# Paged attention with a low-rank layer behind it: value products one pair later, reordered transfers, and 14 of 16 pages on the sync queue

## The chip, the cores and the metric

One NeuronCore of one Trainium2 chip. The time is device microseconds of one execution; less is better. The host only lays arrays out.

## The reference, cut to what matters

```python
# x (32, 32, 512); block table (32, 16) of pages 0..63; cached lengths 207..1644; language ids
B, S, HID = 32, 32, 512;  D, HQ, HK = 128, 32, 8;  PAGES, PSIZE, NPP = 64, 32, 16
q = rope(rmsnorm(x @ Wq.T, q_norm_w), pos);  k = rope(rmsnorm(x @ Wk.T, k_norm_w), pos);  v = x @ Wv.T
kc = k_cache[block_table].reshape(B, 512, HK, D);  vc = v_cache[block_table].reshape(B, 512, HK, D)
k_all, v_all = concat([kc, k], 1), concat([vc, v], 1)          # 544 keys; each KV head serves 4 query heads
scores = einsum('bqhd,bkhd->bhqk', q, k_all) / sqrt(D), cached keys past the length masked
x = x + (softmax(scores) @ v_all).reshape(B, S, HQ * D) @ Wo.T
# second layer: x + x @ W.T + 2 * sum over the top 2 of 8 experts of gate * (x @ A_e.T) @ B_e.T
```

## The kernel before

The 1024 rows of x are cut into 8 tiles of 128 rows (4 batch rows of 32 tokens each), the 8 KV heads into 4 groups of 2. `walk` (L59) runs the same body for each group g and tile t: tiles 0, 6 and 7 are written out, tiles 1 to 5 are a loop, and groups 0 to 2 are a loop around these. So there are 32 bodies, i = 8g + t. In a body there are 8 pairs p (a batch row b = p // 2 and a KV head h = p % 2), each with 4 query heads x 32 tokens = 128 query rows.

Products that need float32 accuracy are made of three passes over operands split into a high and a low part (`three_pass`, L187, whose products all have L193): ACT writes the rounded high part and DVE the rest.

What each engine does in a body:

- PE, for p = 0 to 6: `turn_probs(i, p)` (transposes of the probabilities into PT, L537 and L538), `score(i, p + 2)` into SX, a piece of the projections of the next tile (`fill`: K and V's block 0, query blocks 1 and 2), in some steps a transpose of cached keys (`turn_unit`), of the new queries (`turn_q`) or keys (`turn_k`), then `weigh(i, p)`: eight products of cached values (L550) and two of the tile's own values (L554), which use only the 32 partitions of row b, into O. Then come pair 7 and the output projection `project_out` in two halves, with score 0 and 1 of the next tile between them.
- ACT copies the turned probabilities to SBUF (`take_pT`, L772, one buffer pT), takes exponents (L776), evacuates projections, squares for the norm, and rounds weights (`round_weights`, at the steps of `HI_AT`). It issues 4 of every row's 16 page fetches (L267).
- DVE masks and takes the minimum (L992), normalises (L999), makes the rope products (L975, L979), the low parts of weights at the steps of `LO_AT`, splits O, and adds y (`add_y`, L1027).
- POOL makes the norm factor and finishes the rope (L1258 to L1278), keeps the tile's own values (`keep_v`, L1286), and issues the value gathers, 16 indirect DMAs a tile (L1225).
- SP issues every other transfer, in the written order of its body (L384 to L465): y of the tile (L402), register loads of page addresses (`read_pages`, L319), 12 of every row's 16 key pages for the next tile (`load_pages`, L323 to L326; `fetch_page`, L264), x, masks, halves of weights (`next_half`, L304), cached keys in (`load_kn`) and turned keys out (`store_unit`) for the next group, and last the store of y, for which it waits for `y_added` (L462 to L464).

The cached keys of a group are turned and split once, in 8 units of 8 pages, one unit per tile, and stored to `kT_pages` in DRAM; pages are fetched from there, 64 KB each, by an address in a register. Addresses for all tiles sit in `pages` on one partition, and DVE adds one group's bytes once a group. Row b of the next tile may be fetched once this tile's scores of the row are done (`s_done`). Halves of weights go through two staging buffers.

The order of the work is thus written out by hand: which step each job sits in on each engine, and the order of SP's transfers. All cross-engine order is by semaphores that count up; a queue blocks at the first one that isn't reached.

## Time and profile before

| | us |
|---|---|
| runs shown, median (lowest, highest) | 1611.72 (1608.89, 1619.95) |
| the profiled execution | 1600.16 |
| its span on the engines | 1598.3 |
| PE, POOL, DVE, ACT busy | 1379.9, 948.5, 823.5, 662.0 |
| mean granted TensorE clock | 0.923 of full speed |

The span is from the first to the last instruction of the profiled execution; 1.9 us of its time lie outside. Engine names: PE is TensorE (matmuls), PEld its weight loads, DVE VectorE, ACT ScalarE, POOL GpSimd, SP SyncE; SPq and ACTq are their sequencers, which issue DMAs. "L267" is a line of the kernel above. "xN" is a count, "idle before" the engine's idle time just before an instruction and what ended it. The clock column (PEclk) is a mean of stretches at either 1.0 (2.4 GHz) or 0.5 (1.2 GHz). Waits are put down to what came last.

### The profile page before, as it was taken

Reading aid. Unit: us, or ns where it says so; the run is one execution under the profiler, and the core shown is the slowest. Engines: PE = TensorE matmul, PEld = TensorE weight load, DVE = VectorE, ACT = ScalarE, POOL = GpSimd, SP = SyncE. Lnnn points to the kernel's source line nnn. Section 1 sums busy time; section 2 is a strip of 40 time slices with the busy share of each in tenths; the row PEclk is TensorE's granted clock in tenths of the full one; section 3 lists DMA queues with packets and bytes.
Section 4 is the critical chain, followed back from the end, with each engine's and each line's share of the span. In section 5 each row is a group of like instructions: output and inputs, shape, how many; then the busy total and the mean of one; then the engine's idle time right before and its main releaser. Section 6 shows DMA issues by size and latency. Waiting matters only on the chain.

```text
span 1598.3 us, 33745 instructions
## 1 busy us (share of the span) xinstructions
PE 1379.9 (86%) x8000; PEld 1171.2 (73%) x8000; DVE 823.5 (52%) x2193; ACT 662.0 (41%) x1742; POOL 948.5 (59%) x1270
## 2 busy tenths in 40 slices
PE   4369999998788999999887999999878989888899
PEld 3258787777676777778676787877767877777777
DVE  5445455455455445555545555545545454545544
ACT  3243444444343344444344444444434344434431
POOL 4446666665565667666555666666655666666500
PEclk9588999898999899999898999999879899989999
DMA  8675766678656676677667666667666565656721
GB/s 293 194 211 156 202 193 199 187 202 246 181 177 182 174 201 190 189 200 212 195 178 212 191 199 197 187 191 222 203 197 183 149 182 165 176 168 174 211 77 53
DMA packets 393726, 299.69 MB, mean 187 GB/s; under 512 B 45905, under 2 KB 349297, under 8 KB 393458
## 3 DMA queue, kind: packets, MB, share of 16 engines
q1 hardware_dynamic: 292386, 193.37, 41.3%
q0 software_dynamic: 24576, 67.14, 14.5%
q10 hardware_dynamic: 76656, 37.98, 8.3%
q8 instruction: 38, 0.62, 0.2%
q14 instruction: 70, 0.57, 0.1%
HBM read 271.27 MB, written 29.13 MB: 188 GB/s over the span
## 4 chain that ended last, share of the span: by engine, by line
PE 42%; issue 16%; SPq 15%; DVE 9%; ACT 4%; DMA 4%; another core or an unknown queue 4%; ACTq 3%; POOL 1%; DVEq 0%; POOLq 0%
PE MISC L193 11%; PE O L550 8%; SPq L267 8%; PE SX L193 6%; PE PROJ L193 5%; PE O L554 4%; PE PT L537 4%; DVE soft L992 2%; ACTq L267 2%; ACT pT L772 2%; DMA stage<-in_wqkv 2%; SPq L319 2%; DVE rope_v L979 2%; SPq L266 1%
## 5 line engine op out<-in xcount | busy, mean ns | idle before, releaser
L1225 POOL DMA_INDIRECT v_rows<-in_kv,step_idx x512 | 506.6, 990 | 195.6 <-issue 132.8
L550 PE MATMUL O<-pT,v_rows 128*128 128x128 f32 x2048 | 304.3, 295 | 132.1 <-ACT pT L772 124.6
L776 ACT ACTIVATE soft<-soft,min_all 128x544 f32<-128x544 f32 x256 | 191.7, 749 | 524.0 <-DVE min_all L992 373.3
L550 PEld LDWEIGHTS O<-pT,v_rows 128*128 128x128 f32 x2048 | 276.2, 205 | 173.8 <-ACT pT L772 154.6
L1008 DVE CAST oT_hi<-O 128x128 fp32r<-128x128 f32 x256 | 73.8, 288 | 409.1 <-PE O L554 303.8
L772 ACT ACTIVATE pT<-PT 128x640 f32<-128x640 f32 x256 | 179.7, 702 | 177.6 <-PE PT L538 103.8
L193 PE MATMUL SX<-kT,qT_hi 128*128 128x288 f32 (+1 forms) x1024 | 242.5, 327 | 8.0 <-DVE qT_lo L1021 3.9
L992 DVE CUSTOM_DVE_ANT_0 soft<-SX,mask 128x544 f32<-128x544 f32 x256 | 184.4, 720 | 52.2 <-PE SX L193 23.8
L193 PEld LDWEIGHTS SX<-kT,qT_hi 128*128 128x128 f32 x1024 | 170.7, 202 | 17.8 <-issue 6.7
L537 PE MATMUL PT<-ident,soft 128*128 128x128 f32 x1024 | 180.7, 303 | 2.1 <-issue 2.1
L999 DVE TENSOR_SCALAR soft<-soft,rden 128x544 f32<-128x544 f32 x256 | 157.4, 615 | 9.1
L193 PE MATMUL PROJ<-w_hi,x_hi 128*128 128x512 f32 x384 | 152.5, 397 | 7.8 <-ACT raw L739 4.8
L1269 POOL TENSOR_TENSOR rope_u<-rope_u,rope_v 128x512 f32<-128x512 f32 (+1 forms) x96 | 109.2, 1138 | 80.6 <-DVE rope_v L979 80.6
L193 PE MATMUL SX<-kT,qT_lo 128*128 128x288 f32 (+1 forms) x512 | 155.1, 303 | 0.0
L193 PE MATMUL PROJ<-w_hi,x_lo 128*128 128x512 f32 x384 | 151.9, 396 | 0.0
L193 PE MATMUL PROJ<-w_lo,x_hi 128*128 128x512 f32 x384 | 151.7, 395 | 0.0
L537 PEld LDWEIGHTS PT<-ident,soft 128*128 128x128 f32 x1024 | 123.3, 152 | 32.2 <-issue 6.6
L554 PE MATMUL O<-pT,v_new 32*128 32x128 f32 x512 | 132.2, 340 | 0.0
L1258 POOL TENSOR_SCALAR meansq<-sumsq 128x4 f32<-128x4 f32 (+1 forms) x96 | 23.1, 240 | 158.9 <-ACT squares L746 128.6
L193 PE MATMUL MISC<-wo_hi,oT_hi 128*128 128x512 f32 x256 | 113.0, 441 | 3.7 <-DVE oT_lo L1010 3.6
L193 PE MATMUL MISC<-wo_lo,oT_hi 128*128 128x512 f32 x256 | 105.1, 411 | 0.0
L554 PEld LDWEIGHTS O<-pT,v_new 32*128 32x128 f32 x512 | 80.4, 196 | 33.5 <-issue 5.8
(205 smaller groups left out, 2170.0 us busy)
## 6 DMA issues: line engine op xcount, KB each, us to landing
kT<-kT_pages SPq DMA_DIRECT2D x1536, 64.0 KB
kT<-kT_pages ACTq DMA_DIRECT2D x512, 64.0 KB
mask<-mask_rows SPq DMA_DIRECT2D x64, 272.0 KB
kT_pages<-k_split SPq DMA_DIRECT2D x24, 512.0 KB
stage<-in_wqkv SPq DMA_DIRECT2D x22, 512.0 KB
x_raw<-in_xT SPq DMA_DIRECT2D x32, 256.0 KB
stage<-in_wo SPq DMA_DIRECT2D x16, 512.0 KB
v_rows<-in_kv,step_idx POOLq DMA_INDIRECT x512
```

The source lines that it names most:

```text
L193: mm = nc.tensor.matmul(out_ps, a, b, start=(c == 0 and k == 0), stop=(c == stop_at and k == 2))
L267: eng.dma_start(kT[:, b, j, :, :, :].rearrange("p z h s -> p (z h s)").bitcast(U8), kT_bytes[bass.ds(at, PAGE_BYTES)].rearrange("(d n) -> ...
L537: nc.tensor.transpose(PT[:, c * P:(c + 1) * P], probs[:, p % 2, c * P:(c + 1) * P], ident[:, :])
L550: nc.tensor.matmul(O[:, 0:P], v_rows[:, b, c, h * D:(h + 1) * D], pT[:, c * P:(c + 1) * P], start=c == 0, stop=False)
L554: nc.tensor.matmul(O[:, 0:P], v_new[rows, cols], pT[rows, L:L + P], start=False, stop=True).then_inc(sm["pv_done"], 1)
L772: nc.scalar.activation(pT[:, :], PT[:, 0:L + P], ACT.Copy).then_inc(sm["pT_ready"], 1)
L776: nc.scalar.activation(probs[:, p % 2, 0:KEYS], scores[:, p % 2, :], ACT.Exp, bias=min_all[:, p:p + 1], scale=-1.0, accum_out=den[:, p:p + ...
L992: V.tensor_tensor_reduce(scores[:, p % 2, :], SX[:, SX_AT[p % 2]:SX_AT[p % 2] + KEYS], mask[:, b, :], 1.0, BIG, ALU.add, ALU.min, min_all[ ...
L999: V.tensor_scalar(probs[:, p % 2, 0:KEYS], probs[:, p % 2, 0:KEYS], rden[:, p:p + 1], None, ALU.mult).then_inc(sm["probs_ready"], 1)
L1008: V.tensor_copy(hi, src).then_inc(sm["o_hi_ready"], 1)
L1225: G.indirect_dma_start(v_rows[:, b, c, :], None, v_half[:, :], bass.IndirectOffsetOnAxis(ap=step_idx[:, b * LC + c:b * LC + c + 1], axis=0 ...
L1269: G.tensor_tensor(rope_u[:, 0:w], rope_u[:, 0:w], rope_v[:, 0:w], ALU.add).then_inc(sm["sum_ready"], 1)
```

## The change

It changes where steps stand and who issues transfers; what is computed stays.

- Value products: `weigh(i, p - 1)` now stands in step p, and `turn_probs(i + 1, 0)` and `score(i + 1, 2)` are taken into the end of body i. pT has two buffers. `project_out` of head 0 is cut in two around the last `weigh`.
- The tile's own values are kept as `v_own`: for each of the 4 rows the values times a row mask (`row_mask`, ones on the 32 partitions of that row), so that their product runs over all 128 partitions.
- SP issues 14 of a row's 16 pages and ACT 2. The addresses of a tile are one line of a list in DRAM (`page_dram`), which SP loads two tiles ahead (`load_list`), and all lists are made at the start (`multiples`).
- SP's body has another order: unit store and key load first, then rows 0 and 1, then y, mask, weights; weight halves 0 and 1 of the next group are fetched at the end of tile 0; half 5 ahead of the pages in tile 7. A unit is turned in step 6 of a tile. `HI_AT` and `LO_AT` move by a step or two.
- The rotated queries share `rope_v`; new keys are turned into PROJ; squares use two buffers of 128; the sign of the rope's sine moved from the table into one `scalar_tensor_tensor`.
- The start: key rows are loaded by SP and first, units 0 to 3 are turned and stored ahead of the projections.

```diff
-SP_PAGES = 12
+SP_PAGES = 14
...
+    page_dram = nc.dram_tensor("page_bytes", (GROUPS * TILES, ROWS * NPP), I32, kind="Internal").ap()
...
-        squares = sb("squares", [P, 512], BF16)
+        squares = sb("squares", [P, 2, D], BF16)
-        q_rot = sb("q_rot", [P, 512])
+        q_rot = rope_v
-        v_new = sb("v_new", [P, GK * D])
+        v_own = sb("v_own", [P, ROWS, GK * D])
-        pT = sb("pT", [P, L + P])
+        pT = sb("pT", [P, 2, L + P])
+        K_NEW = PROJ[:, 0:GK * P]
...
-        HI_AT = ((6, 1), (6, 2), (6, 4), (6, 5), (6, 7), (7, 1), (0, 0), (0, 1), (0, 3), (0, 4))
-        LO_AT = ((6, 2), (6, 3), (6, 5), (6, 6), (7, 0), (7, 2), (0, 1), (0, 2), (0, 4), (0, 5))
+        HI_AT = ((6, 1), (6, 2), (6, 4), (6, 6), (7, 0), (7, 2), (0, 0), (0, 1), (0, 4), (0, 5))
+        LO_AT = ((6, 2), (6, 3), (6, 5), (6, 7), (7, 1), (7, 3), (0, 1), (0, 2), (0, 5), (0, 6))
...
# SP
+            def load_list(i):
+
+                sp.dma_start(pages[:, :], page_dram[bass.ds(i, 1), :]).then_inc(sm["pages_in"], 16)
+
+            def read_pages(i, half):
+
+                sp.wait_ge(sm["pages_in"], (i + 1) * 16)
+                sp.nop(nofuse=True)
+                sp.reg_load(page, pages[0:1, half * 2 * NPP:(half + 1) * 2 * NPP]
+                            .rearrange("a (b j) -> a b j", b=2)[:, :, 0:SP_PAGES])
...
+                if not final:
+                    if fixed and t == 0:
+                        load_kn(n_unit, g + 1, 0)
+                    else:
+                        store_unit(n_unit + t, g + 1, t, False)
+                        if not fixed or t < TILES - 1:
+                            load_kn(n_unit + t + 1, g + 1, t + 1)
+                if fixed and t == TILES - 1 and not final:
+                    next_half(g + 1, 5)
+                if not last:
+                    read_pages(i + 1, 0)
+                    if fixed and t == TILES - 1:
+                        sp.wait_ge(sm["ku_stored"], (g + 2) * 16 * UNITS)
+                    load_pages(i + 1, 0)
+                if not (final and fixed and t >= TILES - 2):
+                    load_x(i + 2, (t + 2) % TILES if fixed else t + 2)
+                if not last:
+                    load_pages(i + 1, 1)
                 sp.wait_ge(sm["y_stored"], (i + 1) * 16)
                 sp.nop(nofuse=True)
                 sp.dma_start(y_tile[:, :], y_rows[bass.ds(t, 1), :, :].rearrange("a p n -> p (a n)")
                              ).then_inc(sm["y_in"], 16)
                 if not last:
+                    load_mask(i + 1, tn, 0)
                 if fixed and t == 0:
                     next_half(g, WO_FIRST + 2)
+                    next_half(g, WO_FIRST + 3)
...
                 if not final and fixed and t == TILES - 2:
                     next_half(g + 1, 2)
...
                 if not last:
+                    read_pages(i + 1, 1)
+                    if not before_last:
+                        sp.wait_ge(sm["pages_read"], i + 2)
+                        sp.nop(nofuse=True)
+                        load_list(i + 2)
                     load_pages(i + 1, 2)
+                if not final and fixed and t == TILES - 2:
+                    next_half(g + 1, 3)
...
+                if fixed and t == 0:
+                    if final:
+                        load_l1(0)
+                        load_l1(1)
+                    else:
+                        next_half(g + 1, 0)
+                        next_half(g + 1, 1)
...
# PE
-                nc.tensor.matmul(O[:, 0:P], v_new[rows, cols], pT[rows, L:L + P], start=False, stop=True
+                nc.tensor.matmul(O[:, 0:P], v_own[:, b, cols], pT[:, p % 2, L:L + P], start=False, stop=True
                                  ).then_inc(sm["pv_done"], 1)
...
+                for p in range(PAIRS - 2):
+                    if p > 0:
+                        turn_probs(i, p)
                         score(i, p + 2)
                     for k, c in fill[p] if not last else []:
                         proj(i + 1, k, (c, 1), wcount)
+                    unit(p)
...
                     if not last and p == 5:
-                        pe.wait_ge(sm["qT_ready"], (i + 1) * GK + 1)
                         turn_k(i + 1)
-                    weigh(i, p)
+                    if p > 0:
+                        weigh(i, p - 1)
+                p = PAIRS - 2
+                turn_probs(i, p)
+                if not last:
+                    score(i + 1, 0)
+                    turn_q(i + 1, 1)
+                unit(p)
+                weigh(i, p - 1)
                 turn_probs(i, PAIRS - 1)
+                if not last:
+                    score(i + 1, 1)
+                weigh(i, p)
+                if not last:
+                    turn_probs(i + 1, 0)
+                    score(i + 1, 2)
...
+                project_out(i, 0, (0, REP // 2), g * HALVES + WO_FIRST + 2)
                 weigh(i, PAIRS - 1)
+                project_out(i, 0, (REP // 2, REP // 2), g * HALVES + WO_FIRST + 2)
+                project_out(i, 1, (0, REP), g * HALVES + WO_FIRST + 2)
...
# ACT
+            def read_pages(i):
+
+                act.wait_ge(sm["pages_in"], (i + 1) * 16)
+                act.nop(nofuse=True)
+                act.reg_load(page, pages[0:1, :].rearrange("a (b j) -> a b j", b=ROWS)[:, :, SP_PAGES:NPP])
+                act.sem_inc(sm["pages_read"], 1)
...
+                    if r >= 2:
+                        act.wait_ge(sm["sq_part"], i * 4 + 2 * k - 2 + r - 1)
...
# DVE
+            def multiples(g):
+
+                V.tensor_scalar(list_of(g), table_i, float(PAGE_BYTES), float(g * PAGES * PAGE_BYTES), ALU.mult, ALU.add
+                                ).then_inc(sm["list_ready"], 1)
...
+                if k != 1:
+                    dve.wait_ge(sm["q_turned"], i * GK + k // 2)
...
+                V.scalar_tensor_tensor(r4(rope_v)[:, :, 0, :], r4(raw)[:, :, 1, :], -1.0,
+                                       table[:, tc + 1:tc + 2, 0:64].to_broadcast([P, n, 64]), ALU.mult, ALU.mult)
...
# POOL
-                G.tensor_copy(v_new[:, :], v_next[:, :]).then_inc(sm["v_new_ready"], 1)
+                shape = [P, ROWS, GK * D]
+                G.tensor_tensor(v_own[:, :, :], v_next[:, :].rearrange("p (a n) -> p a n", a=1).to_broadcast(shape),
+                                row_mask[:, :].rearrange("p (b a) -> p b a", a=1).to_broadcast(shape), ALU.mult
+                                ).then_inc(sm["v_own_ready"], 1)
```

The rotations of the next tile start at steps 1, 2 and 4 on DVE (before 1, 3 and 5), and POOL's gathers for rows 0 to 2 of the next tile stand after its rotations 1 and 2.

## Rows read from the trace of the kernel before

**Rows 1.** The page, first lines: span, and PE's busy time
```profile
span 1598.3 us, 33745 instructions
PE 1379.9 (86%) x8000; PEld 1171.2 (73%) x8000; DVE 823.5 (52%) x2193; ACT 662.0 (41%) x1742; POOL 948.5 (59%) x1270
```

**Rows 2.** Busy time by stretch (us from the start): a middle tile, edges, both ends
```profile
core 0: us, PE busy (x) PEld busy (x) DVE busy (x) ACT busy (x) POOL busy (x), PEclk, DMA share, GB/s
...
225.07:266.90 41.83, 38.90 (x244) 32.83 (x243) 22.87 (x66) 19.28 (x52) 28.69 (x40) 1.00 0.68 199
...
354.35:405.00 50.65, 44.93 (x244) 37.84 (x243) 28.53 (x70) 23.75 (x58) 31.07 (x39) 0.87 0.73 219
...
455.60:510.75 55.15, 44.90 (x254) 38.00 (x255) 27.76 (x71) 23.27 (x58) 30.44 (x40) 0.91 0.66 193
...
1521.50:1551.70 30.20, 28.31 (x182) 23.50 (x181) 13.71 (x43) 10.74 (x21) 1.29 (x2) 1.00 0.29 92
1551.70:1598.30 46.60, 42.53 (x250) 36.08 (x248) 19.77 (x48) 8.99 (x25) 0.00 (x0) 1.00 0.12 46
0.00:139.00 139.00, 74.45 (x344) 61.35 (x345) 66.86 (x157) 44.90 (x111) 65.40 (x102) 0.78 0.72 218
```

**Rows 3.** Waits of PE: total us, times, longest
```profile
PE O L550 <- ACT pT L772: 124.6, 86, 7.6
```

**Rows 4.** Timeline of PE in step 2 of a middle tile: start, us
```profile
896.12 1.06 PE L550 MATMUL O<-pT,v_rows 128*128 128x128 f32 x8
897.11 0.48 PE L554 MATMUL O<-pT,v_new 32*128 32x128 f32 x2
897.52 0.66 PE L537 MATMUL PT<-ident,soft 128*128 128x128 f32 x4
```

**Rows 5.** Waits of SP's queue: total us, times, longest
```profile
SPq L463 <- DVE y_tile L1027: 142.3, 21, 12.6
```

**Rows 6.** Timeline of SP over one middle tile: start, us
```profile
888.47 0.35 SPq L464 DMA_DIRECT2D y_running<-y_tile  x1
890.92 0.16 SPq L402 DMA_DIRECT2D y_tile<-y_running  x1
893.86 5.37 SPq L267 DMA_DIRECT2D kT<-kT_pages  x12
...
901.35 8.00 SPq L267 DMA_DIRECT2D kT<-kT_pages  x12
...
915.24 13.80 SPq L267 DMA_DIRECT2D kT<-kT_pages  x24
929.38 0.33 SPq L333 DMA_DIRECT2D mask<-mask_rows  x1
931.95 0.36 SPq L464 DMA_DIRECT2D y_running<-y_tile  x1
```

**Rows 7.** POOL's gathers: three of the same tile, and the group of all
```profile
898.59 1.07 POOL L1225 DMA_INDIRECT v_rows<-in_kv,step_idx  x1 [0.91 <-POOL step_idx L1232]
...
901.41 0.95 POOL L1225 DMA_INDIRECT v_rows<-in_kv,step_idx  x1 [0.30 <-issue]
902.66 0.95 POOL L1225 DMA_INDIRECT v_rows<-in_kv,step_idx  x1 [0.30 <-issue]
...
L1225 POOL DMA_INDIRECT v_rows<-in_kv,step_idx x512 | 506.6, 990 | 195.6 <-issue 132.8
```

**Rows 8.** Timeline of SP and of ACT in tile 6 of group 0: weight half
```profile
375.15 1.22 SPq L301 DMA_DIRECT2D stage<-in_wqkv  x2
...
382.21 1.06 ACT L782 ACTIVATE w_hi<-stage 128x1024 fp32r<-128x1024 f32 x1 [1.99 <-DMA stage<-in_wqkv]
```

**Rows 9.** Timeline of SP at the start: the first tile's pages
```profile
45.77 5.94 SPq L267 DMA_DIRECT2D kT<-kT_pages  x12
...
54.96 29.11 SPq L267 DMA_DIRECT2D kT<-kT_pages  x36
```

**Rows 10.** Groups of instructions: POOL's product of 1024 columns at the start
```profile
L1293 POOL TENSOR_TENSOR w_lo<-soft,w_hi 128x1024 fp32r<-128x1024 f32 x2 | 4.8, 2381 | 0.2
```

More of the change, by code:

```diff
@@ L535, in turn_probs @@
                 pe.wait_ge(sm["probs_ready"], i * PAIRS + p + 1)
+                if not (isinstance(i, int) and i * PAIRS + p == 0):
+                    pe.wait_ge(sm["pT_ready"], i * PAIRS + p)
                 for c in range(LC):
@@ L594, in body, with unit @@
                         [(2, 0), (2, 1)], [(2, 2), (2, 3)], [], []]
-                for p in range(PAIRS - 1):
-                    turn_probs(i, p)
-                    if p + 2 < PAIRS:
+                def unit(p):
+                    u = unit_at(t, p)
+                    if u is None or final:
+                        return
+                    n = UNITS + g * UNITS + u
+                    pe.wait_ge(sm["kn_in"], (n + 1 - UNITS) * 16)
+                    pe.wait_ge(sm["y_added"], CREDIT + i)
+                    pe.wait_ge(sm["ku_ready"], n)
+                    turn_unit(MISC, kn)
+                for p in range(PAIRS - 2):
+                    if p > 0:
+                        turn_probs(i, p)
                         score(i, p + 2)
@@ L810, in _ @@
             nc.scalar.activation(warm[:, :], minus_half[:, 0:1], ACT.Sin).then_inc(sm["warm"], 1)
+            for u in range(4):
+                startup_unit(u)
+            sines(0, slice(0, 1))
             for half in range(2):
@@ L813, in _ @@
             startup_block(0, lambda half: stage[:, half, :, :])
-            sines(0, slice(0, 1))
-            for u in range(2):
+            for u in range(4, UNITS):
                 startup_unit(u)
@@ L878, in body, with jobs @@
                         load_pages(p // 2, p % 2 * (ACT_PAGES // 2), ACT_PAGES // 2)
[L879 to L887 removed]
+                def jobs(p):
                     u = unit_at(t, p)
@@ L892, in body @@
                         round_weights(g, t, p, final)
+                for p in range(PAIRS - 2):
+                    if p > 0:
+                        take_pT(i, p)
+                    if not last and p == 5:
+                        take_qT(i + 1, 0)
+                        take_kT_new(i + 1)
+                    if p > 0:
+                        exponent(i, p + 2)
+                    next_pages(p)
+                    if not last and p in (0, 2, 4):
+                        take_block(i + 1, p // 2)
+                        square_block(i + 1, p // 2)
+                    jobs(p)
+                p = PAIRS - 2
+                take_pT(i, p)
+                if not last:
+                    take_qT(i + 1, 1)
+                    exponent(i + 1, 0)
+                next_pages(p)
+                jobs(p)
+                take_pT(i, PAIRS - 1)
+                next_pages(PAIRS - 1)
+                if not last:
+                    exponent(i + 1, 1)
+                    take_pT(i + 1, 0)
+                    exponent(i + 1, 2)
+                jobs(PAIRS - 1)
             walk(act, body)
@@ L1107, in body, with jobs @@
                 last = final and fixed and t == TILES - 1
-                for p in range(PAIRS - 2):
-                    normalise(i, p + 1)
-                    if not last and p in BLOCK_AT:
-                        rotate(i + 1, BLOCK_AT.index(p))
-                    minimum(i, p + 2)
-                    if not last and p == 4:
-                        rest_qT(i + 1, 0)
-                    if not last and p == 5:
-                        rest_kT_new(i + 1)
+                def jobs(p):
                     u = unit_at(t, p)
@@ L1325, in body @@
                 keep_v(i)
-                if not last:
-                    make_table(i + 1, tn)
                 b = ROWS - 1
```

415 lines of the change are left out of this document (186 added, 229 removed).

## The prediction

> **What bounds the kernel now.** I read the page first: PE is busy 1379.9 of 1598.3 us [rows 1], so all that the other engines do matters only where PE waits for it. The table by stage comes next [rows 2]. The reader is to see four things in it. A tile in the middle of a group (225.07 to 266.90) lasts 41.83 us, of which PE is busy 38.90 at a granted clock of 1.00 (the 2.4 GHz level). The tiles at a group's edge (354.35 and 455.60) last 50.65 and 55.15 us, busy 44.93 and 44.90, with the clock at 0.87 and 0.91: there PE idles 5.7 and 10.3 us and part of the work runs at the 1.2 GHz level. The last tile takes 30.20, the second layer behind it 46.60, and everything up to the end of the first tile 139.00 us with PE busy 74.45. So 30 tiles lie between 139 and 1521.5 us, 46.1 us each.
>
> The waits of PE [rows 3]: 124.6 us in 86 waits is value products (L550) waiting for ACT's copy of the turned probabilities (L772). That is what the change's "one pair behind" is aimed at. The timeline of PE [rows 4] prices the new-row product: 8 products on 128 rows start at 896.12, the two on 32 rows at 897.11, the next transpose at 897.52. The two take 0.41 us, and the eight 0.99, with 0.2 of it the step into the 32-row form ((1.06 - 0.275)/7 is 0.112 us for one in the stream).
>
> Then I asked which queue has room for more. SP waits for y_added at L463 142.3 us in 21 waits, at most 12.6 [rows 5]; that is nearly all the slack it has. Its timeline of one tile [rows 6] runs from the store at 888.47 to the next one at 931.95, 43.48 us. It waits about 1.7 us for the stored y (888.8 to 890.9, less the loop's own instructions) and 2.2 us at the end (929.7 to 931.95). So SP works or is held in issuing for 39.6 of 43.5 us. Its 48 page fetches take 5.37 + 8.00 + 13.80 = 27.17 us, 0.566 us each. **The sync queue is almost as full as PE**, which PE's own waits don't show.
>
> **The change, part by part.**
>
> Own rows as a 128-row product: per pair 2 products at 0.112 in place of 0.41, and the step of about 0.09 ahead of them goes too: 0.28 us x 8 pairs = 2.3 us of PE per tile. A middle tile's PE work is 38.9 - 2.3 = 36.6 us. In return POOL writes 128x1024 masked values instead of copying a quarter as many. The nearest row of that size took 2.38 us [rows 10], so up to 2.4 us more on POOL, once a tile, ahead of the last row's gathers and of ACT's v_next. Behind it wait ACT's copy of v_next (about 7 us of PE work later) and the value products of the next tile's pair 0, two slots on. It is hidden; if not, at most 2.4 us a tile.
>
> Value products one pair behind: ACT's copy of pair p now has the next turn, score and projection steps to run beside, some 3 us of PE work. The 124.6 us go, and with them the drops to the 1.2 GHz level that follow them. What is late next: the new-key turn (now behind block 2's evacuation, and score 0 behind its two splits) and the second query turn. Both have about 1 us less room than they need, so I leave 1.5 us of PE idle per tile. PE alone would then want about 39 us in a middle tile.
>
> The rope, squares and table edits (in-place rotated block, two squares buffers, one scalar_tensor_tensor in place of a tensor_tensor): bounded by -0.3 and +1 us a tile, on DVE and ACT, which are busy 22.87 and 19.28 of 41.83 us [rows 2]. I take 0, since PE has them beside it; the waits that they add (DVE behind q_turned before block 2, ACT behind its own square) sit in those 1.5 us.
>
> **Pages: 14 of 16 on SP.** ACT loses 8 issues a tile, about 4 us of its sequencer, ahead of its copies; that only helps PE. SP gains 8 issues and one list fetch. What does one issue cost? The first 12 went out in 5.37 us (0.45 each) and the next 12 in 8.00 (0.67) [rows 6]. The difference is what lies beside them [rows 7]: from 898.59 on POOL generates descriptors for its gathers, and SP's issues stretch. The gathers stay at 16 a tile, 506.6 us in all, so SP's loss per tile stays or grows a little as SP works on through times in which it used to wait. Bounds for the 8: 3.6 us (0.45) and 5.4 us (0.67). I take the mean, 0.566, so 4.5 us, and 0.5 us for the list (an issue of 0.35 with its register work). The wait for the stored y goes, since two rows of pages now stand ahead of it. SP per middle tile: 39.6 + 4.5 + 0.5 = 44.6; I use 44.5, against 39 for PE. **So SP takes over as the bound.** The slack ahead of it is small: row 1's pages are now needed at the end of the same tile (score of pair 2 of the next tile is in the last slot), not in the next one, so SP can lag some 5 us before PE waits at L527's scores. After that the tiles follow SP. In the last group no unit is stored or loaded, two issues fewer with their register work and waits, an estimated 1.5 to 3 us: I take 42.
>
> The Trainium skill's page "DMA: Bandwidth & Descriptors" (Issuing engines are not separate DMA queues) says that a choice of issuing engine only moves sequencer time, usually small beside the transfer; by it the move would cost nothing, and PE would bound (the first rival below). The Trainium skill's page "Perfetto Trace Analysis" (DMA Optimizations) advises balancing issues over the engines when descriptor generation looks like the limit, which speaks against putting them on one. The trace agrees with the second: 27 of 43 us are page issues [rows 6].
>
> Group edges. In tile 6 the third half of weights is fetched behind two rows of pages. It was issued from 375.15 [rows 8], 20.7 us after the tile's start, and ACT sat idle 1.99 us for it until 382.21, so it lands some 6 us on. Now 4 pages more stand ahead of it and two weight issues fewer, so it is issued at about 21.5 plus SP's lag and lands at 27.5 or later, while ACT's slot comes earlier by the 3 to 4 us that PE saves. ACT waits 5 to 10 us there and PE most of it: tile 6 stays at 50. Tile 7 loses its long wait (its half is now ahead of the pages): 45. Tile 0 has two output halves behind two rows of pages, and SP two weight halves more at its end: 48.5 (46 in the last group).
>
> Start. SP issued its first page at 45.77 and the 36 of rows 1 to 3 took 29.11 us [rows 9]. The key rows and units now go first, which may bring the first page 3 to 4 us forward; the list has to be written to DRAM and read back, some 4 us beside the same stores. 16 pages more stand on SP by the end of tile 0 (9 us), less what SP waited for y at that end (up to the 12.6 of rows 5). I take 134 for 139, between 125 and 150.
>
> **Sum.** 134 + group 0 (5 x 44.5 + 50 + 45 = 317.5) + groups 1 and 2 (2 x (48.5 + 317.5) = 732) + group 3 (46 + 6 x 42 = 298) = 1481.5. The last tile 30.2 - 2.3 - 0.4 = 27.5, the second layer 46.6 as before: span 1555.6, 43 us less than 1598.3. The profiled execution took 1600.16 us, 1.9 over its span; the median of the runs shown is 1611.72, a factor of 1.0072. 1557.5 x 1.0072 = 1569; I round down a little for ACT's relief: 1566.
>
> **Rivals.**
> 1. SP's extra issues don't bind (it catches up, or issues faster without ACT's beside them), and PE bounds. For it: SP shows waits in nearly every tile. Against: those waits are 2 to 4 us in middle tiles, and 5 us are added. 20 middle tiles x 39 + 3 x (47 + 43 + 45) + 40 = 1225, + 134 + 27.5 + 46.6 = 1433 span, 1445 us.
> 2. The weights' waits at the edges and SP's load add instead of covering each other, and the mean page issue is 0.59 rather than 0.566: 56 x 0.024 x 30 = 40 us more, 1606 us: within 1% of before.
> 3. The sync queue issues at the pace seen beside the gathers, since it is now never idle while they run. At 0.67 for all 56 pages a tile is 39.6 - 27.2 + 37.5 + 0.5 = 50.4 us; 30 tiles x 5.9 us more gives a span of 1733, 1747 us. It decides early: 42.7 us over 30 tiles and 56 pages is 0.025 us, so from a mean of 0.59 us the gain is gone, and from about 0.603 it is slower by over 1%. For it: 12 pages at 0.67 [rows 6]. Against: the gathers come 1.25 us apart [rows 7], 16 of them take 20 us of each tile, and the rest goes at 0.45.
> 4. The lag of a pair does nothing for PE, because the waits move to other steps. PE's mean tile is then 46.1 - 2.3 = 43.8 us, just under SP's mean of 44.9 (1347.5 / 30), so the time is the forecast's or up to 20 us more; it would show in PE's waits, where L550 still waits for L772.
>
> **How the numbers follow.** Forecast (with rival 4, whose time is close) 0.58, rival 1 0.14, rival 2 0.17, rival 3 0.11, mostly near its threshold rather than at its full price. What a measurement of this kernel can tell from no change is about 1%, so faster means under 1595.6 and slower over 1627.8. Faster: 0.14 + nearly all of 0.58 = 0.70; same 0.19; slower 0.11. The range of 0.8 leaves out the full forms of rivals 1 and 3: 1495 to 1622. SP at 42.5 us a tile gives 1506, at 46 about 1612.
>
> **What would show it.** Right: SP's queue without waits at the y_added wait in middle tiles; tiles of 43 to 46 us there; PE waiting for DMA kT<-kT_pages at the scores of the last two slots, absent before; the wait of L550's successor for pT under 20 us; PE's busy time down by about 70 us for the 32-row products; ACT waiting for stage in tile 6. Wrong: SP still waits at y_added by over 3 us a tile (then PE or another engine bounds, and the time is under 1500 if it's PE); or page issues at 0.60 us and more in the mean (then it is no gain). Of the steps, the page issue's mean cost is the one that the time hangs on.

## The result, and the profile after

| | before, us | after, us |
|---|---|---|
| runs, median (lowest, highest) | 1610.31 (1600.05, 1619.95), 4 runs | 1685.11 (1675.12, 1687.34), 4 runs |
| profiled execution, its span | 1600.16, 1598.3 | 1686.77, 1685.0 |
| mean granted clock | 0.923 | 0.901 |

The ratio is 1.0453, 95% interval 1.0375 to 1.0532: slower, where 1566 us was forecast. The page after, and the table by stage (start, the 30 tiles between, last tile and second layer; each row has the stretch, its length, the busy time of PE, PEld, DVE, ACT and POOL, the granted clock, the DMA share and GB/s), against the 139.00, 1382.5 and 76.8 us that the same stages took before:

```profile
span 1685.0 us, 34346 instructions
...
PE 1306.1 (78%) x8000; PEld 1159.5 (69%) x8000; DVE 865.3 (51%) x2195; ACT 652.1 (39%) x1741; POOL 980.3 (58%) x1264
```
```profile
0.00:131.00 131.00, 66.09 (x352) 56.21 (x353) 71.95 (x166) 46.70 (x113) 68.29 (x98) 0.79 0.76 228
131.00:1613.80 1482.80, 1174.22 (x7233) 1045.99 (x7232) 761.16 (x1945) 587.72 (x1587) 909.31 (x1164) 0.91 0.62 179
1613.80:1685.00 71.20, 65.83 (x419) 57.30 (x418) 32.17 (x87) 17.68 (x42) 2.66 (x3) 1.00 0.20 71
```

The ends are a little shorter; the loss is all in the middle, 100 us more in the same 30 tiles, although PE is busy 60 us less there (1234.6 before). So PE's idle time there went from 148 to 309 us. Its waits over the whole run say where:

```profile
PE MISC L194 <- DVE oT_lo L1078: 77.5, 22, 7.1
PE MISC L194 <- issue: 44.6, 16, 4.2
PE PT L577 <- issue: 40.9, 11, 10.1
PE SX L194 <- DVE kT L1082: 40.3, 23, 2.8
PE PT L577 <- ACT pT L827: 38.9, 7, 12.5
PE PROJ L547 <- POOL rope_v L1360: 31.8, 17, 6.1
```

The 124.6 us of [rows 3] are gone from the value products as meant; 38.9 us of waiting for the same copy stand at the turns instead, nearly all of it in tiles 0 and 6 of a group. In their place stand 122 us at MISC, the output projection, 77.5 of them put down to DVE's oT_lo. DVE is not busy then. One such wait, in a tile of group 2, on PE, DVE, ACT and POOL (start, us):

```profile
1160.18 0.39 PE L593 MATMUL O<-pT,v_own 128*128 128x128 f32 x2
...
1163.48 0.28 PE L194 MATMUL SX<-kT,qT_lo 128*128 128x256 f32 x1
1169.44 0.76 PE L194 MATMUL MISC<-wo_hi,oT_hi 128*128 128x512 f32 x1 [5.68 <-DVE oT_lo L1078]
1170.00 0.63 PE L194 MATMUL MISC<-wo_lo,oT_hi 128*128 128x512 f32 x1
1170.43 0.63 PE L194 MATMUL MISC<-wo_hi,oT_lo 128*128 128x512 f32 x1
```
```profile
1168.68 0.29 DVE L1076 CAST oT_hi<-O 128x128 fp32r<-128x128 f32 x1 [5.59 <-remote]
```
```profile
1168.74 0.70 ACT L827 ACTIVATE pT<-PT 128x640 f32<-128x640 f32 x1 [4.78 <-remote]
```
```profile
1157.21 1.07 POOL L1308 DMA_INDIRECT v_rows<-in_kv,step_idx  x1 [0.17 <-issue]
...
1166.11 0.95 POOL L1308 DMA_INDIRECT v_rows<-in_kv,step_idx  x1 [0.30 <-issue]
```

Before has bursts of four only, but for the first tile's twelve: row 0's, 1's and 2's gathers each stood behind a rotation of their own. The change puts row 1's behind rotation 2 next to row 2's, with the eight small operations of POOL's table ahead of both, and this makes one burst of eight in 24 of 31 tiles.

A second cost is in the rows from 1170.00: products of 128x512 follow each other 0.43 us apart, and 0.23 us where PE has not idled (in the trace of after_again below). The granted clock is 0.50, the 1.2 GHz level, from 1167.2 to 1174.0, so after the wait of 5.68 us PE works 4.6 us more at half speed.

### The profile page after: what moved, and what is told of

It is laid out like the page before. It is cut to its first block, busy times and chain, and to the rows that moved or that the text cites. A ratio compares the mean times of both kernels' runs of the same rounds, so it can differ in the third digit from the quotient of the medians.

```text
span 1685.0 us, 34346 instructions
## 1 busy us (share of the span) xinstructions
PE 1306.1 (78%) x8000; PEld 1159.5 (69%) x8000; DVE 865.3 (51%) x2195; ACT 652.1 (39%) x1741; POOL 980.3 (58%) x1264
## 4 chain that ended last, share of the span: by engine, by line
PE 30%; SPq 22%; issue 18%; DVE 9%; another core or an unknown queue 7%; POOL 6%; DMA 4%; ACT 2%; ACTq 1%; DVEq 0%; POOLq 0%
SPq L278 13%; PE MISC L194 9%; PE O L591 5%; PE PROJ L194 5%; PE SX L194 5%; SPq L345 4%; POOL v_rows L1308 2%; PE PT L577 2%; DVE soft L1067 2%; DVE soft L1060 2%; SPq L277 2%; POOL rope_u L1351 1%; DMA mask<-mask_rows 1%; PE O L593 1%
## 5 line engine op out<-in xcount | busy, mean ns | idle before, releaser
L1308 POOL DMA_INDIRECT v_rows<-in_kv,step_idx x512 | 513.3, 1003 | 229.6 <-issue 130.9
L591 PEld LDWEIGHTS O<-pT,v_rows 128*128 128x128 f32 x2048 | 290.8, 212 | 29.6 <-issue 16.5
L194 PE MATMUL SX<-kT,qT_hi 128*128 128x288 f32 (+1 forms) x1024 | 238.5, 322 | 74.1 <-DVE kT L1082 40.3
L577 PE MATMUL PT<-ident,soft 128*128 128x128 f32 x1024 | 162.1, 283 | 89.8 <-issue 40.9
L194 PE MATMUL MISC<-wo_hi,oT_hi 128*128 128x512 f32 x256 | 119.1, 465 | 122.2 <-DVE oT_lo L1078 77.5
L1067 DVE TENSOR_SCALAR soft<-soft,rden 128x544 f32<-128x544 f32 x256 | 178.8, 698 | 9.1
L1340 POOL TENSOR_SCALAR meansq<-sumsq 128x4 f32<-128x4 f32 (+1 forms) x96 | 18.9, 197 | 231.2 <-ACT squares L799 203.9
L194 PEld LDWEIGHTS MISC<-wo_hi,oT_hi 128*128 128x128 f32 x256 | 54.4, 212 | 141.4 <-issue 132.3
L1370 POOL TENSOR_TENSOR v_own<-v_next,row_mask 128x1024 f32<-128x1024 f32 x32 | 60.5, 1889 | 123.0 <-PE O L593 108.8
L785 ACT ACTIVATE raw<-PROJ 128x256 f32<-128x256 f32 x32 | 12.3, 385 | 282.5 <-PE PROJ L194 184.3
```

The lines of the kernel that those rows point to most:

```text
L194: mm = nc.tensor.matmul(out_ps, a, b, start=(c == 0 and k == 0), stop=(c == stop_at and k == 2))
L577: nc.tensor.transpose(PT[:, c * P:(c + 1) * P], probs[:, p % 2, c * P:(c + 1) * P], ident[:, :])
L591: nc.tensor.matmul(O[:, 0:P], v_rows[:, b, c, cols], pT[:, p % 2, c * P:(c + 1) * P], start=c == 0, stop=False)
L1067: V.tensor_scalar(probs[:, p % 2, 0:KEYS], probs[:, p % 2, 0:KEYS], rden[:, p:p + 1], None, ALU.mult).then_inc(sm["probs_ready"], 1)
L1308: G.indirect_dma_start(v_rows[:, b, c, :], None, v_half[:, :], bass.IndirectOffsetOnAxis(ap=step_idx[:, b * LC + c:b * LC + c + 1], axis=0 ...
```

## The experiments

Ratios are against runs of the kernel before on the same chip. The 18 runs fell on six chips of two kinds, which matters about as much as the largest edit: on three of them, and where the change was first timed, before takes 1610 to 1628 us, on the three others 1523 to 1524. "Chip of the first kind" and "second kind" below are these. Runs 1 to 12 were all on the first kind and 13 to 18, later on, all on the second. Where two runs on different chips of one kind are compared, it is by their ratios, each of which has its interval beside it.

**1 and 2. Gathers apart (after_apart), and 12 pages (after_sp12).** The two suspects, one at a time.

```diff
# after_apart: POOL's body, row 0's gathers ahead of rotation 1, row 1's ahead of rotation 2
                 for k in range(2):
                     make_rstd(i + 1, k)
                     rotate_sum(i + 1, k)
+                    ...
+                    next_values(k)
...
-                next_values(0)
                 make_rstd(i + 1, 2)
...
-                next_values(1)
                 next_values(2)
# after_sp12
-SP_PAGES = 14
+SP_PAGES = 12
```

> The changed kernel with POOL's gathers put apart again: row 0's behind rotation 0, row 1's behind rotation 1, row 2's behind rotation 2, as in the kernel before; 14 pages on SP stay. Gather theory: in the changed kernel's trace PE's semaphore updates arrive late only while POOL issues gathers, a median of 0.64 us after the matmul's end in runs of 4 gathers and 4.6 us (up to 8) in runs of 8, of which there is one per tile just where DVE and ACT wait for PE; with no runs of 8 some 4 to 5 us a tile go, 1545 to 1580 us. Queue theory (SP with 14 pages is the bound, as the prediction had it): SP's work per tile doesn't change, so 1660 to 1690 us.

> The changed kernel with 12 pages on SP and 4 on ACT, nothing else. Queue theory: 8 issues of 0.6 us go from SP in each of 30 tiles, so up to 145 us, 1540 to 1580 us. Gather theory: PE still gets the late updates, and only what SP's lateness adds to it (mask 0, weights at the group's edges) goes: 1640 to 1680 us.

Measured: 1717.89 us, 1.0567 (1.0505 to 1.0629), and 1709.52 us, 1.0556 (1.0492 to 1.0621). Each lies above what either theory expected. After_sp12 still has the bursts of eight, with 4.9 us of lag in them, and the largest wait is the same:

```profile
PE MISC L194 <- DVE oT_lo L1078: 88.0, 22, 7.2
```

SP now waits 208.5 us at y_added, so it has time; it buys nothing while PE stands still for another reason. After_apart has no burst of eight, and the wait for oT_lo fell to 24.0 us. But two others took its place:

```profile
PE PROJ L547 <- POOL rope_v L1360: 119.1, 27, 5.2
PE MISC L547 <- POOL rope_v L1360: 109.8, 31, 7.9
```

In the changed order a row's values are weighed a pair later, so gathers put ahead of a rotation make it wait for pv_done (between 500 and 1300 us POOL's gathers wait 167.5 us for PE's value products, 29.1 in the changed kernel), and PE's query turns wait for the rotation. The edit had a price of its own. So after_apart decides nothing on the bursts. After_sp12 does tell against the queue as the only bound, and says nothing on what it costs once the other cause is gone.

**3 and 4. Both (after_apart_sp12), and the pages alone in the old kernel (before_sp14).**

> Both: gathers apart and 12 pages on SP. If the two causes are separate, their gains add: about 1480 to 1530 us, under both kernels. If only one is real, this is the same as the one that carries it, within 15 us.

> The kernel before with 14 pages on SP, nothing else. Queue theory: SP worked 38 us of 46 a tile and gets 4.7 us more, so its slack is used up and in middle tiles (39.6 of 43.5 us) it passes the tile's length by 1 us: 1615 to 1660 us. Gather theory: no more than 10 us from the kernel before, 1600 to 1620 us.

Measured: 1701.96, 1.0488 (1.0426 to 1.055): the rotations' waits again, 8.1 us of a middle tile. And 1716.23, 1.0557 (1.0483 to 1.0631): two pages of 16 more on SP cost the old kernel 94 us. Its middle tiles go from 43.9 to 46.4 us (mean of the same ten), but in groups 0 to 2 the tiles numbered 6 go from 49 to 51 up to 61 to 64 us and the tiles numbered 0 from 54 or 55 to 61, where the weights queue behind the pages (ACT's waits for halves of the projections' weights go from 25.9 to 73.2 us); L550's wait for pT rises from 124.6 to 198.8 us. So the queue is a bound of its own in the old order, and dearer at the edges than I had it.

**5 to 7. The burst cut without a price of its own.** The table, 2.3 us of small operations, moves between row 1's gathers and row 2's (after_split); with 12 pages (after_split_sp12); with the first mask half ahead of row 1's pages too (after_split_sp12_mask).

```diff
+                next_values(1)
                 if not (final and fixed and t == TILES - 2):
                     make_table(i + 2, (t + 2) % TILES if fixed else t + 2)
-                next_values(1)
                 next_values(2)
```

> The changed kernel with one step moved on POOL: the table of the next tile but one (8 small operations, 2.3 us) is made between the gathers of row 1 and those of row 2, not ahead of both, so that the two rows' gathers are bursts of 4 with a gap and no longer one burst of 8. Nothing else is touched. Burst theory (TensorE's completions reach the other engines 4.6 us late while POOL issues 8 gathers back to back, 0.6 us late in a burst of 4; the 4.4 us per middle tile that PE waits for oT_lo ahead of the output projection are that): the wait goes to 1 to 2 us, middle tiles from 48.3 to 45.5 to 47, where the sync queue's 46 us of work hold them, and the run to a ratio of 1.01 to 1.03 against before. Order theory (the wait for oT_lo comes from the new order of the products, whatever the gathers do): the wait stays at 4 us and the ratio at 1.04 to 1.055.

> As after_split, and 12 of 16 pages on the sync queue, 4 on the scalar engine's, as before. Burst theory: with neither the burst of 8 nor the longer queue, middle tiles have PE's 38 us and 5 to 6 of waits, 43.5 to 45, ratio 0.97 to 1.01. Queue theory alone (what is late is the sync queue's transfers): not below after_split by more than 1%, since 12 pages alone gave nothing. Order theory: ratio 1.04 to 1.055 again.

> As after_split_sp12, with the load of the first mask half put ahead of row 1's pages on the sync queue, where before it stood behind them and the load of y. If VectorE's wait for that mask (3.7 us of a middle tile in the changed kernel) is on the path, the time falls by 15 to 60 us below after_split_sp12; if VectorE has that time to spare, within 8 us of it.

Measured: 1636.41, **1.0037** (1.001 to 1.0064); 1568.71, **0.9593** (0.9523 to 0.9662); 1562.96, 0.9588 (0.9527 to 0.9649). One line moved on POOL takes back the 4 points, and the wait for oT_lo falls from 77.5 to

```profile
PE MISC L194 <- DVE oT_lo L1078: 24.0, 19, 1.8
```

In after_split SP does not wait for y_added in any of the 15 middle tiles of the first three groups: with 14 pages the queue is full there. Now, and only now, 12 pages are worth something: 4.4 points. Middle tiles (mean of the ten) are 48.3, 46.0 and 44.1 us in after, after_split and after_split_sp12. VectorE's wait for the mask was to spare: moving it gave nothing that shows. Of the 60 us that after_split_sp12 lies under before on its chip, 15 are the start (the first tile ends at 123.0 and not at 138.2 us) and 6 the last tile (24.7 and 30.3). A middle tile of 44.1 us is no shorter than before's 43.9, but those two traces are from different chips, on which before takes 1628 and 1610 us.

**8. The burst alone, in the old kernel (before_together).** Row 1's gathers move from behind rotation 1 to behind rotation 2, next to row 2's.

> The kernel before, with one step moved on POOL: the gathers of row 1 are not issued behind rotation 1 but with those of row 2 behind rotation 2, so that there is a burst of 8 in each tile. Burst theory: PE's completions in that stretch come 4 to 5 us late, pT, O and the scores with them, and a tile grows by 1.5 to 4.5 us: 1660 to 1750 us. Order theory (bursts of 8 cost nothing, since the wait in the changed kernel has another cause): within 1% of before.

Measured: 1736.37, 1.0648 (1.0579 to 1.0717), 108 us more. The lag in the bursts of eight is 1.24 us in the median (0.5 to 1.9 with other rules for pairing), a tenth over 3.4 to 3.7, and a wait of 3.6 us in the old kernel is now

```profile
PE MISC L193 <- DVE oT_lo L1010: 60.8, 29, 5.4
```

The order of the products is the old one here, so the loss belongs to the gathers. That row 1's values are fetched later has no price of its own that shows: PE waits 12.4 us for v_rows here and 12.3 in before.

**9 and 10. What the 128-row product is worth.** In after_split_sp12 taken back (after_split_sp12_row32), and in the old kernel put in alone, which leaves out the masking of the other rows' values (before_rows128).

```diff
# after_split_sp12_row32
+                rows = slice(b * SEQ, (b + 1) * SEQ)
-                nc.tensor.matmul(O[:, 0:P], v_own[:, b, cols], pT[:, p % 2, L:L + P], ...
+                nc.tensor.matmul(O[:, 0:P], v_own[rows, b, cols], pT[rows, p % 2, L:L + P], ...
# before_rows128
-                nc.tensor.matmul(O[:, 0:P], v_new[rows, cols], pT[rows, L:L + P], ...
+                nc.tensor.matmul(O[:, 0:P], v_new[:, cols], pT[:, L:L + P], ...
```

> As after_split_sp12 (ratio 0.959), but the product of a row's own values takes the row's 32 partitions again and not 128 with zeros; the result is the same. The traces have that step at 0.28 us more of PE for each of 256 pairs, 2.3 us a tile. If PE's time is the path there, the run comes 50 to 75 us above after_split_sp12, ratio 0.99 to 1.005; if its steps hide in the waits for late completions, under 25 us above it.

> The kernel before with one change: the product of a row's own values takes all 128 partitions of the last probability block and of the new values. It leaves out the masking, so that a row's sum also takes in values of other rows; the work of PE is the changed kernel's, and POOL's 1.5 us more per tile for the masked copy is left out. PE's busy time falls by 70 us. With PE as the path that is 45 to 70 us of the run, 1560 to 1585 us by a before of 1628; if pT and the completions hold the tile, under 20 us.

Measured: 1590.26, 0.982 (0.9773 to 0.9867), against 0.959 with 128 rows; and 1584.07, 0.9787 (0.974 to 0.9833). PE's busy time is 1349.3 us with 32 rows and 1276.2 in after_split_sp12, at granted clocks of 0.935 and 0.932: 73 us, of which the run shows some 2.2 points, 36 us. In the old kernel the run moves by as much, 2.1 points. So half of the step's work is time; the rest goes into waits.

After_split_sp12_row32 also shows what the rest of the change is worth: it has neither the 128-row product nor the bursts of eight nor the two pages more on SP, and it is 1.8% under before. Of these 27 us, 15 are the start: its first tile ends at 123.2 us, and at 138.0 in before_rows128 on the same chip, which has the old start. Another 4 are the last tile (26.4 and 30.3 in before). The 30 tiles between take 1392 us, against 1382.5 in before on a chip that is 0.4% faster. So on this kind of chip it is not shown that the lag of a pair shortens a middle tile.

**11. The burst broken up (after_split_sp12_mask_fine).** The table's eight operations go two by two between the four gathers of row 1.

> As after_split_sp12_mask (ratio 0.959), and the four gathers of row 1 are not back to back: between two of them POOL makes two of the eight small operations of the table (0.6 us), so the number of operations stays and only the burst is broken up. If PE's completions are let through wherever POOL is not issuing a gather, their lag in that stretch (1.0 us median in bursts of 4, up to 3.3) falls under 0.9 us at most and the 1.9 us that PE waits at pair 6's product goes to under 1: a tile 0.8 to 1.5 us shorter, 1525 to 1545 us. If the lag comes from the gathers' descriptors being worked off, not from the issue, 0.6 us of pause changes nothing: within 8 us.

Measured: 1502.98, **0.9301** (0.9243 to 0.9359), 2.9 points under after_split_sp12_mask, where 1 to 2 were expected. PE's idle time in a middle tile falls from 6.3 to 4.5 us, nearly all of it at the value products (L590, 3.0 to 1.1). POOL's timeline in one tile, row 1 apart and row 2 in a row:

```profile
1022.64 0.98 POOL L1307 DMA_INDIRECT v_rows<-in_kv,step_idx  x1 [0.16 <-issue]
1023.64 0.33 POOL L1326 TENSOR_TENSOR table<-cos,norm_w 128x64 f32<-128x64 f32 x1
1023.92 0.32 POOL L1328 TENSOR_TENSOR table<-sin,norm_w 128x64 f32<-128x64 f32 x1
1024.40 0.98 POOL L1307 DMA_INDIRECT v_rows<-in_kv,step_idx  x1 [0.16 <-PE O L592]
...
1029.24 1.18 POOL L1307 DMA_INDIRECT v_rows<-in_kv,step_idx  x1 [0.30 <-issue]
1030.73 0.94 POOL L1307 DMA_INDIRECT v_rows<-in_kv,step_idx  x1 [0.30 <-issue]
```

Of the completions of PE that fall to such single gathers, over 100, the lag is 14 ns in the median and 0.23 us at most; in the rows that still go in fours it is 0.6 to 1.7 us by the rule for pairing, up to over 3. It is the gathers in a row that hold PE's completions back. With 0.8 us from one's end to the next one's start, 0.6 of it small operations, they get through; with 0.3 us of nothing they mostly don't. The other theory of the expectation, in which a pause changes nothing, is out. But the last rises come 1.5 us and more behind a burst of eight, so the end of the issue alone doesn't free them; how the gathers hold them is open.

**12. An early wait on ACT (after_split_sp12_mask_ku).** In tile 7 ACT copies the projection's first block before it waits for the stored keys.

> As after_split_sp12_mask, and in a group's last tile the scalar engine copies the first block of the projection before it waits for the last unit of keys to be stored, not after it. PE's 5.3 to 5.5 us of wait for v_next in tiles 7 of the first three groups is that wait: 10 to 16 us less in all if nothing else is late there, none if the weights' rounding takes its place.

Measured: 1550.28, 0.959 (0.9534 to 0.9645), ratio unchanged. In the first group's tile 7 PE's wait of 5.5 us for v_next is gone, and the tile takes 48.5 us where it took 50.5; whether the run gains 10 us by it, these rounds can't tell.

**13 to 18. The second kind of chip.** The next six runs were meant to part queue and burst further: after_fine (the changed kernel, 14 pages, row 1's gathers apart) and one_between_sp12 (12 pages, the mask and ACT edits, one table operation in each gap of rows 1 and 2).

> The changed kernel with all 14 pages on the sync queue; only POOL's order is changed: the four gathers of row 1 with two table operations between each two, and so no burst of 8. If the sync queue is a bound of its own (46 us of work a middle tile, late weights in tile 6), the run stays at a ratio of 0.99 to 1.005, as after_split (1.004) though the lag is smaller; if the queue only showed because of the bursts, it falls to 0.94 to 0.96.

> As after_split_sp12_mask_ku (0.959, no wait for the stored keys ahead of the first copy), with the eight small operations of the table one by one between the gathers of row 1 and of row 2, so that each gap has 0.3 us and no burst is left in either row. If 0.3 us lets PE's completions through as 0.6 us does (14 ns median), both rows gain: 1470 to 1500 us, ratio 0.91 to 0.93. If it is too short, the two rows are one burst of 8 as in the changed kernel: 1600 us or more.

They ran where before takes 1523.53 us: 1507.03, 0.9896 (0.9834 to 0.9957), and 1439.34, 0.9472 (0.9413 to 0.953). In both traces no completion of PE is late: wherever the rise can be paired, it comes 16 ns behind at most. So the changed kernel itself was run again (after_again), on a second such chip:

> The changed kernel as it is. Where PE's completions come late under bursts of gathers (before at 1610 to 1628 us): ratio 1.04 to 1.055 as the first time. Where they don't (before at 1523 us): no wait for oT_lo ahead of the output projection, middle tiles 41 to 43 us with the sync queue as the bound, ratio 0.98 to 1.01. If the loss had nothing to do with late completions it would be over 1.03 there too.

Measured: 1509.24, **0.9892** (0.9862 to 0.9922): there the change is faster. Its trace has not one "remote" wait on any engine, and in its bursts of eight the lag is 14 ns. It has the bursts of eight, after_fine has row 1's gathers apart, and the two take 0.989 and 0.990 of before: where no completion is late, breaking the bursts up buys nothing. That is the control for the runs above. The stretch that stood still above, with the same eight gathers beside it:

```profile
1028.41 0.39 PE L593 MATMUL O<-pT,v_own 128*128 128x128 f32 x2
...
1032.35 0.39 PE L194 MATMUL MISC<-wo_hi,oT_hi 128*128 128x512 f32 x1
1032.58 0.39 PE L194 MATMUL MISC<-wo_lo,oT_hi 128*128 128x512 f32 x1
1032.81 0.40 PE L194 MATMUL MISC<-wo_hi,oT_lo 128*128 128x512 f32 x1
```
```profile
1027.55 1.07 POOL L1308 DMA_INDIRECT v_rows<-in_kv,step_idx  x1 [0.17 <-issue]
...
1035.20 0.95 POOL L1308 DMA_INDIRECT v_rows<-in_kv,step_idx  x1 [0.30 <-PE O L593]
```

POOL issues at the same pace, 1.25 us a gather, on both. SP does not. The fetches of rows 2 and 3 in a middle tile, on the second kind and, below it, on the first:

```profile
1027.06 13.93 SPq L278 DMA_DIRECT2D kT<-kT_pages  x28
```
```profile
1156.34 19.12 SPq L278 DMA_DIRECT2D kT<-kT_pages  x28
```

That is 0.50 against 0.68 us a page beside the same gathers. Over the runs the mean from one page's issue to the next is 0.53 us on the second kind whether gathers run or not, and on the first 0.54 away from them and 0.74 beside them, 0.62 in all. (Waits between two pages count in these means; the median is 0.49 us on both.) So what [rows 6, 7] show of SP's stretching, and PE's late completions, come and go together.

The last three runs were meant for the first kind of chip and met the second: after_fine again (after_fine_again) 1509.04, 0.9915 (0.9876 to 0.9953), one_between_sp12 twice more (one_between_again, one_between_third), 1429.55, 0.9385 (0.9333 to 0.9438), and 1434.85, 0.9427 (0.9363 to 0.9492). Against after_fine they are 4 to 5 points lower with 12 pages in place of 14, and three small edits (the mask, the ACT wait, the gaps in row 2). The mask and the ACT wait gave nothing on the first kind, so most of it is likely the queue; no run here has the pages alone on the second kind.

> The version with one small operation in each gap between the gathers of rows 1 and 2, and 12 pages. It was 0.947 of before where completions are not late. Where they are: if 0.3 us between two gathers lets them through, their median lag in those rows is 14 ns as with 0.6 us, and the ratio is 0.90 to 0.93; if it is too short, the two rows act as a burst of 8, with a ratio over 0.98.

So three things are open. Whether one operation of 0.3 us between two gathers is pause enough on a chip of the first kind was not seen. Whether the kind is a property of the chip, or of something in its state when the runs were made, can't be told from six chips with one visit each, the first kind's all before the second's. And why PE's rises alone are held, no run tells.

## Why the prediction was wrong

Its direction holds on the second kind of chip (0.989, the forecast was 0.972) and fails on the kind on which both kernels had been timed. Point by point:

- **Own rows as a 128-row product.** PE is busy 73.8 us less (1379.9 to 1306.1), with the clock lower. The clean pair, with and without the step at nearly the same clock, has 73 us, as worked out (2.3 us a tile, "about 70"). Right; but of such work about half turned into time.
- **Value products one pair behind.** The 124.6 us went, right. What I put in their place was 1.5 us of PE idle per tile. Measured was 9.1 us of a middle tile (3.2 in before), 4.8 of it at the output projection, 1.7 at the scores for new keys and 1.2 at the query turn. On the second kind it is 3.5 us, 2.6 of it rotation 2 behind row 0's gathers. This is the term that failed.
- **The step that was missing** is that POOL's order was left without a price: "The gathers stay at 16 a tile, 506.6 us in all, so SP's loss per tile stays or grows a little". Their number stayed, their grouping did not: two fours became an eight, since row 1's gathers came to stand next to row 2's. After_split puts that at 4 points, before_together at 6.5 points in the old kernel. It could have been asked for: 113 us of waits for "remote" stood in the trace before, on engines that had nothing remote, 107 of them beside gathers or up to 1.6 us behind.
- **SP takes over as the bound.** True on the second kind: there SP waits 0.05 us at y_added in each of the 15 middle tiles of the first three groups (1.4 to 3.4 in most of the last, where it has no units to store), and middle tiles are 40.6 us, not 44.5, because a page costs 0.53 and not 0.566 us. On the first kind it was one of two bounds, and not the later one: 12 pages gave nothing with the bursts in place, 4.4 points without them. The page's mean there was 0.62 us (0.58 over the whole trace of before, where the prediction took 0.566 from one tile), beyond the 0.603 at which rival 3 said the change turns slower. Rival 3 had the right side and a true part of the price; alone it would have given about 0.054 x 56 x 30 = 90 us over the forecast, 1656 us by the forecast's own sum. But it was not what held the tile, since after_sp12 takes those pages away and stays at 1.056. On the second kind the forecast had the right bound and too large a gain, 0.972 for 0.989; of the middle tiles it had asked too much, of tiles 6, 7 and 0 too little.
- **The moved issues.** The Trainium skill's page "DMA: Bandwidth & Descriptors" (Issuing engines are not separate DMA queues), by which the choice only moves sequencer time, usually small beside the transfer, is half borne out here: it is sequencer time that moves, but with 56 pages a tile that is not small, and before_sp14 is 5.6% slower for 8 issues a tile.
- **Ends and edges.** First tile's end 134, measured 131.0. Last tile 27.5, measured 24.6. Tail 46.6, measured 46.5. Tile 6 50, measured 51 to 52. Tile 7 45, measured 56 to 58: I had dropped the weights' wait but had not seen that ACT stands at that tile's head for the last stored keys, with its copy of the first block behind it (5.5 us of PE in after_split_sp12_mask), nor the late completions. Tile 0 48.5, measured 53 to 54.
- **Signs.** Of those I had named as right, PE's busy time, the vanished wait of the value products for pT, the wait for tile 6's weights (PE waits 9 to 11 us behind it in the first three groups' tiles 6 on the second kind) and the shrinking of SP's at y_added (142.3 to 67.3 us, 72.4 on the second kind) came true. Tiles of 43 to 46 us did not on either, and PE never waited for kT pages outside the start: an engine can run full and the one that depends on it still be held by something else. The sign of being wrong, page issues at 0.60 us and more in the mean, came true on the first kind (0.62).

## What to carry to other kernels

When a change touches a queue, write down for each engine which of its own instructions now stand next to each other, not only how many there are: here two rows' gathers that came to stand next to each other cost 4 points, and one table put between them took these back. If a single-core trace has waits put down to something remote, look what another engine was issuing at that time, and break such bursts with work that must be done anyway. Before ruling a cause out because removing it gave nothing, remove it once more with the others gone, and note which chip each run was on.

## What the runs showed of the hardware

- On chips of the first kind PE's semaphore increments are held back while POOL issues indirect gathers in a row: 0.5 to 2 us in the median in bursts of four, by run and by rule for pairing; in bursts of eight 4.5 us and more in the changed kernel and 0.5 to 1.9 in before_together. The last of them come 0.6 to 1.1 us behind a burst of four and 1.5 to 1.9 us behind one of eight. With 0.6 us of small operations between two gathers it is 14 ns. Increments of DVE, ACT and POOL are not held (8 to 13 ns).
- This is so on some chips, or in some state of them, and not on others (there 14 ns in bursts of eight too). The others also issue a page in 0.53 us beside gathers, not 0.74, and run the kernel before in 1523 instead of 1610 to 1628 us. A kernel tuned on one kind can come out on the other side of a change on the other: 1.045 and 0.989 for the same code.
- The fastest versions seen are after_split_sp12_mask_fine, 0.930 of before on the first kind, and one_between_sp12, 0.94 to 0.95 on the second; neither was run on the other kind.
